# Three narrow attentions: ScalarE issues part of the second batch's copies, the third batch's projection comes earlier and has a bank of its own, and there are three scratch buffers in DRAM

## What is computed

```python
q = (query @ Wq.T + bq).reshape(b, tq, NUM_HEADS, HEAD_DIM).transpose(0, 2, 1, 3)
k = (key @ Wk.T + bk).reshape(b, tk, NUM_HEADS, HEAD_DIM).transpose(0, 2, 1, 3)
v = (value @ Wv.T + bv).reshape(b, tk, NUM_HEADS, HEAD_DIM).transpose(0, 2, 1, 3)
scores = jnp.einsum('bhqd,bhkd->bhqk', q, k) / np.sqrt(HEAD_DIM)
attn = jax.nn.softmax(scores, axis=-1)
out = jnp.einsum('bhqk,bhkd->bhqd', attn, v)
return out.transpose(0, 2, 1, 3).reshape(b, tq, EMBED_DIM) @ Wo.T + bo
```

## Time and profile before

| | us |
|---|---|
| median of 3 runs | 2174.31 (2173.11 to 2175.66) |
| the profiled execution | 2182.17 |
| its span in the trace | 2180.4 |

### The profile page before, as it was taken

The page is one execution under the profiler, slowest core; times in us unless marked ns, Lnnn a source line. Parts: engine busy times, 40 slices in busy tenths (PEclk is TensorE's granted clock), DMA queues, the critical chain, the costliest instruction groups (busy, mean ns, idle before and its releaser), DMA issues.

```text
span 2180.4 us, 37976 instructions
## 1 busy us (share of the span) xinstructions
PE 1875.8 (86%) x13416; PEld 1265.7 (58%) x13416; DVE 1526.5 (70%) x3631; ACT 1310.5 (60%) x2803; POOL 588.6 (27%) x569
## 2 busy tenths in 40 slices
PE   7999776997999999968977488999997997779886
PEld 4777564445777777644444254666665676534465
DVE  5777677866777677547848848899997456678533
ACT  5777533775878888735765656776665212357622
POOL 3223003102544443414001003444343001221043
PEclk9999997998999999978998699999999998889898
DMA  4000003411000000006302000000001000363202
GB/s 202 2 2 2 1 1 119 138 55 39 1 2 1 1 1 1 1 15 196 102 1 80 0 1 1 1 1 1 1 2 39 20 1 1 117 180 112 59 25 80
DMA packets 80156, 87.40 MB, mean 40 GB/s; under 512 B 6579, under 2 KB 70116, under 8 KB 79074
## 3 DMA queue, kind: packets, MB, share of 16 engines
q1 hardware_dynamic: 78625, 82.49, 11.9%
q0 software_dynamic: 1344, 2.49, 0.4%
HBM read 54.39 MB, written 30.70 MB: 39 GB/s over the span
## 4 chain that ended last, share of the span: by engine, by line
PE 52%; DVE 28%; ACT 8%; issue 6%; POOL 3%; DMA 2%; SPq 1%; DVEq 0%; POOLq 0%; ACTq 0%
PE bank L469 44%; DVE scratch L1269 4%; PE bank L653 2%; ACT XN L2059 2%; DVE scratch L3134 2%; DVE scratch L3154 2%; PE bank L3016 2%; PE bank L368 2%; PE bank L693 1%; DVE stats L245 1%; DVE XN L3174 1%; DVE scratch L1671 1%; DVE w_keep L1958 1%; ACT L2137 1%; PE bank L1238 1%
## 5 line engine op out<-in xcount | busy, mean ns | idle before, releaser
L469 PE MATMUL bank<-scratch 64*128 64x256 bf16 (+6 forms) x2936 | 307.7, 303 | 34.5 <-DMA scratch<-parts 13.5
L1269 DVE TENSOR_REDUCE scratch<-bank 128x2 f32<-128x512 f32 x384 | 243.1, 685 | 59.8 <-PE bank L469 59.2
L469 PE MATMUL bank<-w_keep,scratch 128*128 128x128 f32 (+4 forms) x1760 | 243.1, 329 | 19.2 <-DVE scratch L2001 4.0
L469 PEld LDWEIGHTS bank<-scratch 64*128 64x128 bf16 (+4 forms) x2936 | 177.3, 123 | 139.0 <-DVE scratch L1269 44.6
L1355 ACT ACTIVATE w_keep<-bank 128x512 f32<-128x512 f32 x384 | 212.4, 597 | 71.3 <-PE bank L469 63.6
L469 PE MATMUL bank<-XNT,w_keep 128*128 128x256 f32 (+4 forms) x800 | 236.9, 435 | 6.5 <-POOL w_keep L2198 5.5
L469 PEld LDWEIGHTS bank<-w_keep,scratch 128*128 128x128 f32 (+3 forms) x1760 | 181.7, 184 | 84.0 <-issue 54.8
L469 PE MATMUL bank<-w_early,scratch 64*128 64x256 f32 (+3 forms) x1152 | 163.3, 344 | 24.0 <-ACT w_early L3234 8.7
L469 PEld LDWEIGHTS bank<-XNT,w_keep 128*128 128x128 f32 x800 | 149.7, 196 | 58.0 <-issue 28.3
L469 PEld LDWEIGHTS bank<-w_early,scratch 64*128 64x128 f32 (+3 forms) x1152 | 119.0, 183 | 69.1 <-issue 28.5
L469 PE MATMUL bank<-w_keep 128*32 128x256 f32 (+2 forms) x1728 | 141.0, 389 | 13.3 <-ACT w_keep L1355 5.4
(11 more groups left out here) (461 smaller groups left out, 3852.0 us busy)
## 6 DMA issues: line engine op xcount, KB each, us to landing
scratch<-parts SPq DMA_DIRECT2D x24, 1024.0 KB, 5.2
parts<-scratch SPq DMA_DIRECT2D x192, 96.0 KB, 2.8
parts<-scratch SPq DMA_DIRECT2D x96, 64.0 KB, 2.1
w_early<-pack_l3f SPq DMA_DIRECT2D x1, 5206.0 KB, 15.4
w_keep<-pack_l2f SPq DMA_DIRECT2D x1, 2124.0 KB, 13.3
w_early<-pack_mamba SPq DMA_DIRECT2D x1, 2120.0 KB, 18.6
w_keep<-pack_l2x SPq DMA_DIRECT2D x1, 2049.0 KB, 8.6
w_keep<-taps SPq DMA_DIRECT2D x4, 512.0 KB, 6.4
```

Of the source, the lines that this page charges most:

```text
L469: return pe.matmul(out, lhsT, rhs, start=start, stop=stop, skip_group_check=True)
L1269: dve.tensor_reduce(neg[:, :, h], self.compare_bank(g)[:, :].rearrange("p (t s) -> p t s", s=S), AXX, ALU.max, negate=True).then_inc(*s.ma ...
```

## The change

- ScalarE issues, in all three attentions, the eight writes of batch 1's parts 0 and 1 and the reads of batches 0 and 1. They stand in its queue at the new step `EARLY` = -15, behind the masks of batch 1. SP keeps batch 0's 12 writes, batch 1's four of part 2, and everything from batch 2 on.
- The projection of batch 2 moves from step -8 to step -15 and goes to bank 3 instead of bank 7; it waits for neither `emptied` nor for the cut of batch 0.
- The first 20 compares get banks by a table, `ROTATION`: 4, 5, 0, 1, 2 in turn up to the 14th, then 4, 5, 2, 3, 4, 5; the 18th (bank 3) waits until ScalarE has read the projection from bank 3. The softmax products of heads 2 and 3 now wait for the maxima of the compares that used banks 2 and 3.
- There are three DRAM buffers, so the writes of batch b wait for the read of batch b-3.
- The bias additions on GpSimd move two batches later, behind the cut of batch 3 (`raw_attention`: of batch 4).

```diff
@@ class Narrow
+    ROTATION = (4, 5, 0, 1, 2, 4, 5, 0, 1, 2, 4, 5, 0, 1, 4, 5, 2, 3, 4, 5)
     FIRST = -24
+    EARLY, EARLY_PLACE = FIRST + H // 2 + 1, FIRST + H
@@ compare_bank, reused
-        return self.k.bank[(4, 5, 0, 1, 2, 3)[m % 6] if m < H else 4 + m % 2]
+        return self.k.bank[self.ROTATION[m] if m < self.DIRECT else 4 + m % 2]
-        m = y ^ 1
-        m -= 6 if m < H else 2
-        return m ^ 1
+        bank, before = self.compare_bank(y), (y ^ 1) - 1
+        while before >= 0 and self.compare_bank(before ^ 1) is not bank:
+            before -= 1
+        return before ^ 1 if before >= 0 else None
@@ other
+        if p in (self.EARLY, self.EARLY_PLACE):
+            return ("project", 2) if p == self.EARLY and self.projection is not None else None
@@ weigh_and_compare_pe
                 if g >= 4:
                     pe.wait_ge(*s.weighed.at("e", g - 4))
+                elif g >= 2:
+                    pe.wait_ge(*s.maxed.at("x", 14 + g))
...
-            if compares and 2 <= y ^ 1 < 6:
+            if compares and 2 <= y ^ 1 < 5:
                 pe.wait_ge(*self.turned_at((y ^ 1) - 2))
+            if compares and y ^ 1 == 17 and self.projection is not None:
+                pe.wait_ge(*s.stacked.at("project", 2))
@@ project_bank, other_pe
-        return self.k.bank[6 if b == 1 else 7]
+        return self.k.bank[{1: 6, 2: 3}.get(b, 7)]
-        if (kind, b) != ("project", 1):
+        if kind != "project" or b > 2:
             self.emptied(pe, p)
-            for q in {0: (0,), 2: (1, 2, 3)}.get(b, ()):
+            for q in {0: (0,), 2: (1, 3), 3: (2,)}.get(b, ()):
@@ act
-                if b >= 2:
+                if b >= 3:
                     act.wait_ge(*s.pool.at("cut", b - 2, 3))
...
+            if p == self.EARLY:
+                for c in range(2):
+                    self.spread(act, 1, c)
+                for b in range(2):
+                    self.gather(act, b)
@@ spread
-        s, dram, wide = self.k.s, self.k.parts_dram[b % 2], H // 2 * S
+        s, dram, wide = self.k.s, self.k.parts_dram[b % 3], H // 2 * S
+    def gather(self, e, b):
+        s, dram, wide = self.k.s, self.k.parts_dram[b % 3], H // 2 * S
+        e.wait_ge(*s.parts_out[b % 2].at(b))
+        e.dma_start(self.stacks[b % 3].rearrange("p (n x) -> p n x", n=2),
+                    bass.AP(dram.tensor, dram.offset, [[wide, P], [P * wide, 2], [1, wide]])).then_inc(*s.loaded_stack(b % 3).up(b))
@@ sync
-            if b >= 2:
-                sp.wait_ge(*s.loaded_stack((b - 2) % 3).at(b - 2))
-            for c in range(3):
+            if b >= 3:
+                sp.wait_ge(*s.loaded_stack(b % 3).at(b - 3))
+            for c in range(2 if b == 1 else 0, 3):
                 self.spread(sp, b, c)
             if b >= 3:
                 sp.wait_ge(*s.scored.at("s", (b - 2) * H - 1))
-            sp.wait_ge(*s.parts_out[b % 2].at(b))
-            sp.dma_start(...)
+            if b >= 2:
+                self.gather(sp, b)
@@ pool of raw_attention; of guarded_attention and heads_of_hybrid
-            if b == 2:
+            if b == 4:
-            if b == 1:
+            if b == 3:
```

More of the change, by code:

```diff
@@ L1177, in weigh_and_compare_pe @@
             g, y = a + i, x + 1 - i
-            if compares and self.reused(y) >= 0:
+            if compares and self.reused(y) is not None:
                 pe.wait_ge(*s.maxed.at("x", self.reused(y)))
-            if compares and 2 <= y ^ 1 < 6:
+            if compares and 2 <= y ^ 1 < 5:
                 pe.wait_ge(*self.turned_at((y ^ 1) - 2))
+            if compares and y ^ 1 == 17 and self.projection is not None:
+                pe.wait_ge(*s.stacked.at("project", 2))
             for c in range(HALVES):
@@ L1456, in spread @@
                 e.dma_start(place, part).then_inc(*s.parts_out[b % 2].up(*((b,) if (c, n, o) == (2, 1, 1) else (b, c, n, o))))
+    def gather(self, e, b):
[3 more added lines that the diff above has]
+                    bass.AP(dram.tensor, dram.offset, [[wide, P], [P * wide, 2], [1, wide]])).then_inc(*s.loaded_stack(b % 3).up(b))
     def sync(self, sp):
-        k, s, wide = self.k, self.k.s, H // 2 * S
+        s = self.k.s
         for b in range(B):
-            dram = k.parts_dram[b % 2]
-            if b >= 2:
-                sp.wait_ge(*s.loaded_stack((b - 2) % 3).at(b - 2))
-            for c in range(3):
+            if b >= 3:
+                sp.wait_ge(*s.loaded_stack(b % 3).at(b - 3))
+            for c in range(2 if b == 1 else 0, 3):
                 self.spread(sp, b, c)
@@ L1469, in sync @@
                 sp.wait_ge(*s.scored.at("s", (b - 2) * H - 1))
-            sp.wait_ge(*s.parts_out[b % 2].at(b))
-            sp.dma_start(self.stacks[b % 3].rearrange("p (n x) -> p n x", n=2),
-                         bass.AP(dram.tensor, dram.offset, [[wide, P], [P * wide, 2], [1, wide]])).then_inc(*s.loaded_stack(b % 3).up(b))
+            if b >= 2:
+                self.gather(sp, b)
 def raw_attention(k):
@@ L4306, in build @@
         k.kern_dram = dram["wave_kernels"]
-        k.parts_dram = [nc.dram_tensor(f"parts_{n}", [2 * P, H // 2 * S], BF16, kind="Internal").ap() for n in range(2)]
+        k.parts_dram = [nc.dram_tensor(f"parts_{n}", [2 * P, H // 2 * S], BF16, kind="Internal").ap() for n in range(3)]
         walk(k, lambda name, program: program(Null()))
```

## The result

| | us |
|---|---|
| median of before, beside the changed kernel | 2174.98 (6 runs) |
| median of the changed kernel | 2166.78 (6 runs, 2165.32 to 2167.92) |
| ratio | 0.9963, interval 0.9951 to 0.9974 |
| the profiled execution, its span | 2165.32, 2163.5 |

The change makes the kernel 8.2 us faster (by the interval 5.7 to 10.7). The forecast was 13.6 us.

The account below looks back on a forecast made before the run. TensorE's three step-0 waits, 13.5 us, were put down to 24 writes issued on SP's one queue. Gains of 5.0 + (1.4 + 0.3 + 1.0) + 5.9 = 13.6 us gave 2160.7 us, range 2154.5 to 2169.5.

Parts of the forecast that it names:

- the rival of the DMA engines: Step 0, all attentions: DMA engines become the limit, last writes land after 6.5 us; 3.6 us gained, 2170.7 us; chance 0.07.
- The issues: ScalarE's queue: eight writes at 0.66 us each from about 351.4 in the first attention, 5.3 us in all.
- the first rival: SP and ScalarE take turns issuing, one issue per 0.65 us for both; 0.6 us gained, 2173.7 us; chance 0.07.
- the one with slow issues: ScalarE's writes: gains reach zero at 1.39 us each; at 1.67 us, 6.7 us slower, 2181.0 us; chance 0.04.
- The landing of batch 1's last write: Before read 1, from issue to landing: 3.7 us in the first attention, 2.9 us in the other two.
- The landing of read 1: Batch 1's read ahead of step 0: 5.3 us in all three attentions.
- The second attention: Gain there: 1.4 us for the whole wait, 0.3 us for compares, 1.0 us for an earlier clock rise.
- The clock in the other two: TensorE's clock in first and third attention: no gain counted, since a gap of 1 to 2 us is left.
- The parts put at zero: Earlier projection counted as zero; TensorE ready up to 1 us earlier through the later bias, counted as nothing where batch 1 decides.
- ScalarE's blocking costs nothing: Behind ScalarE's reads stands only the copy of batch 0's negated maxima, needed at step 0, where TensorE needs batch 1 anyway.
- VectorE's cut shorter: Sign in the trace after: VectorE's cut in the first attention takes less than 3 us.
- The collision: First and third attention: GpSimd's later bias overlaps VectorE's cut of batch 1, up to 2 us more each; 2164.7 us; chance 0.04.

Follow-up runs that it names:

- read 0 last: Changed kernel, but ScalarE issues read 1 and then read 0, both after batch 1's last write has landed; ratio to the kernel before 0.9962.
- both held: Changed kernel, but ScalarE issues read 1 before read 0, and SP starts batch 2's writes only after batch 1's have landed; ratio to before 0.9955.

## Why the prediction was right, and where its sizes were off

**The sign and the mechanism** were right: the chain of issue times was the limit, splitting it over two queues shortens it, and the gain needs ScalarE's DMAs (without them 0.9996 or 1.0035). The time, 2166.78, is within the range; the sum was 5.4 us too large. It was not a close forecast. The 8.2 us lie below the 9 to 20 us that the prediction called its own bounds, and the time is nearer to the 2170.7 of the rival of the DMA engines than to the forecast's 2160.7. Of its signs, the waits near 1.5 and below 1 us at step 0 did not come (4.67 and 4.52), and a landing of 5 us and more, which was to mean that rival, did. That the range held owes something to its width.

**The issues** were right to some tenths: 0.642 us each against the 0.66 taken, ScalarE's first at 351.53 against 351.4, SP's last of batch 1 at 14.1 us after the start of the stage against 14.6. The two queues don't take turns, so the first rival and the one with slow issues fell.

**The landing of batch 1's last write is the term that was mis-sized.** 3.7 us (first) and 2.9 us (second, third) were taken; it was 5.7, 6.3 and 5.6. It was issued within 0.2 us of read 0 in all three attentions and landed within 0.3 us of that read. Holding read 0 back brought it to 2.1 to 2.5 us with the engines as full. The 3.7 was a median over eight writes issued behind a read the earlier trace rows, and the row that mattered is inside it. In the kernel before, the first of the eight, issued 0.43 us behind the read on the same queue, took 5.0 us:

```profile
parts<-scratch SPq DMA_DIRECT2D x1, 96.0 KB, 5.0
```

So this was there to be read before. **The landing of read 1** was the second: 5.3 taken from the earlier trace rows, 6.1, 5.5 and 5.9 measured, 5.3 again in the first attention when batch 2's writes were held. The restarts came 2.6 us earlier than before instead of 5.0 in the first and 2.2 instead of 5.9 in the third attention.

**The rival of the DMA engines** had the right term and nearly its size: landing at 6.5 us, the longest row, gave 2.2 and 2.3 us for the first and the third attention, and 2.6 and 2.2 were measured. Its reason, engines that are full, is not enough, as the run with read 0 last shows. In the second it forecast a loss of 0.9 us. That missed because ScalarE's DMAs started at 977.16, against the 983.44 taken, of which only 2.1 us are the earlier start of the stage: they stand behind the masks in the code but were issued beside them, so there was time for a slow landing.

The Trainium skill ("DMA: Bandwidth & Descriptors", section "Issuing engines are not separate DMA queues") says that DMAs of several engines run on the same 16 DMA engines and interleave, and that only the sequencer's time is saved. The prediction argued against "usually small" from the issue times and was right that they counted: without the second queue nothing is gained. It passed over the first half of the rule. The trace agrees with it on the shared engines (their share went from 0.21 to 0.97, with packets of both queues). But from 360 to 363 us only the read's queue moved anything.

**The second attention** gained 1.8 us against 2.7. Its wait for a DMA is gone as forecast, but the restart moved by 0.85 us, not 1.4 + 0.3: VectorE's cut of batch 0's maxima is 1.2 us longer, and TensorE's restart then waits 0.44 us for VectorE. The clock still falls, and is at the low level from about 17 to 24 us after the start (before: 14 to 28). With read 0 last it is low for only some 3 us, from 17 on, and the stage is 136.07 us; with both held 135.84. The restart comes 1.3 and 1.7 us earlier there too, so what the clock alone is worth was not separated. Half of the 3.4 us less at the low level is 1.7 us (an estimate), about the 1 to 2 us that the prediction put at stake.

**The clock in the other two** was put at nothing, and was not nothing. In the third attention the clock rises 31.7 us after the start before and 31.5 after (worked out from the share of the low level in these slices), though the restart is 2.2 us earlier:

```profile
1927.00:1928.00 1.00, 1.00 (x10) 0.64 (x6) 0.76 (x2) 0.88 (x3) 0.71 (x2) 0.85 0.27 66
```

```profile
1921.00:1922.00 1.00, 1.00 (x11) 0.48 (x10) 0.43 (x2) 0.04 (x1) 0.94 (x2) 0.70 0.36 92
```

So 1.9 us more of TensorE's work behind the restart fell to the low level, which costs about half of that (the eight products of a step take 1.04 us at the low level, at 370.48, and 0.60 at the high, at 375.95): 2.2 - 1.0 = 1.2 us as an estimate, 1.1 measured. In the first attention the clock is low for 0.9 us less behind the restart: 2.6 + 0.5 = 3.1, 3.0 measured.

**The parts put at zero** were at zero in sum only. The earlier projection is not free work moved about: without it ScalarE's reads block the copy and the whole is slower (1.0022). "ScalarE's blocking costs nothing" held for the changed kernel (24.2 us of waiting at L1391, none on the path) because that copy had gone ahead. "VectorE's cut shorter" was wrong: in the first attention its first row took 1.14 us beside GpSimd, against 0.94 before, since GpSimd's cut of batch 2 now waits 3.97 us for writes to land and starts at 358.63, again beside VectorE; the whole cut took 3.3 us against 3.1. **The collision** of bias and cut was a rival on the first and third attention; it showed in the second, and only where SP issues all.

**What stays open.** In the third attention the clock is low until 31 us after the start before and after, and in the kernels with the restart at 24.4 to 25.3 until 28. What decides between 28 and 31 was not separated from the restart. Why SP's queue stands still while the read moves is open too. Whether read 0 issued only some 0.7 us later would be enough was not tried, nor whether fewer bytes written would shorten the chain.

None of the variants with ScalarE's DMAs and the early projection can be told from the changed kernel: the lowest ratios, 0.9954 and 0.9955, lie within each other's intervals and its own. Every order of the same bytes restarts TensorE 24.4 to 26.3 us after the start of the first and the third attention. The forecast had 23.6 and 21.7, the best runs 24.8 and 24.4: of its 13.6 us some 4 were to be had by none of them.

## What to carry to other kernels

A chain of small DMA issues on one queue is worth splitting. But a landing time has to be read from the row that stands as the new one will stand: a median over writes at different distances behind a read hides the one right behind it. A read that is not needed first, issued together with the last write of what is needed, delays that write until the read has landed, on the same queue or on another; issue it behind, and then count the bytes, since of two reads at once the second pays. Whoever moves blocking waits onto a compute engine has to clear first what stands behind them in its queue, and work on GpSimd that is moved, or held up by a late landing, has to be placed by what VectorE does at that time in every variant of the stage. And an earlier restart at the low clock is worth less than its length.

## What the runs showed of the hardware

- Two queues issue writes side by side, most at 0.60 to 0.66 us each, with no sign of taking turns. Some are stretched: three in a row to 0.8 to 0.9 us on SP and two on ScalarE in the third attention, one on each to 1.4 us in the first; single ones of 1.3 to 1.7 us stand on SP in the kernel before too.
- Writes of 64x3x256 and 64x2x256 bf16 from two queues keep the DMA engines at a share of 0.97 with 245 GB/s moved; two reads of 1 MB, with some writes among them, reach 357 to 395 GB/s at a share of 1.02 to 1.07.
- A 64 KB write that landed in 2.1 to 2.5 us without a read took 5.7, 6.3 and 5.6 us with a 1 MB read issued within 0.2 us of it on another queue, and a write issued 0.6 us ahead of the read 2.2 us. Behind a read on the same queue, by 0.43 us, one of 96 KB took 5.0.
- Two 1 MB reads issued 0.5 us apart landed in 5.3 to 5.4 and 8.1 to 8.2 us, where one alone takes 5.3 (first attention).
- ScalarE's DMA issues ran beside its own activations ahead of them in the code: in the second attention the first went out at 977.16, and the ten masks before it start at 977.22. An activation behind its DMAs waited for their waits (12.41 us).
- VectorE's rows of 0.20 us took 0.67 to 1.20 us beside GpSimd's additions.
